# A fused attention and mixture-of-experts layer: other VectorE steps in the routing, places in a group's fourth tile, the fifth group's shared rows in the middle stage, and sums in halves at the end

## What is computed

```python
q = layernorm(x)                                   # eps 1e-5
out = attention(q Wq, ctx Wk, ctx Wv; 16 heads of 64) @ Wo + bo
x = x + (gamma * norm(q + out, eps=1e-3) + beta)
f = layernorm(x)                                   # 4096 tokens
scores = softmax(f @ Wg)                           # 32 experts
weights, indices = top_k(scores, 4)
for e in range(32):                                # at most C = 4 * (4096 * 4) / 32 pairs
    y[tok_e] += silu(f[tok_e] W1[e]) * (f[tok_e] W3[e]) @ W2[e] * w_e    # hidden size 128
z = silu(f Ws1) * (f Ws3) @ Ws2                    # shared, hidden size 256
return x + y + z
```

## Time and profile before

| | before |
|---|---|
| median of 3 runs | 789.82 us (789.68 to 792.14) |
| profiled execution: time, span | 792.1 us, 790.3 us |
| mean TensorE clock granted | 0.981 |
| TensorE matmul, weight load busy | 747.7 us (95%), 596.3 us (75%) |
| VectorE, ScalarE, GpSimd busy | 533.0 us (67%), 465.4 us (59%), 379.6 us (48%) |
| DMA | 164.44 MB, mean 208 GB/s |
| instructions | 18644 |

### The profile page before, as it was taken

One profiled execution on the slowest core, in us unless ns is written; L12 is line 12 of the kernel. 1 busy time (PEld: TensorE's weight loads), 2 busy tenths in 40 slices (PEclk: granted clock), 3 DMA queues, 4 the chain that ended last, 5 costly groups with the idle time before them and its releaser, 6 DMA issues.

```text
span 790.3 us, 18644 instructions
## 1 busy us (share of the span) xinstructions
PE 747.7 (95%) x4222; PEld 596.3 (75%) x4223; DVE 533.0 (67%) x1683; ACT 465.4 (59%) x1820; POOL 379.6 (48%) x352
## 2 busy tenths in 40 slices
PE   6988999999999999999998959999999999999995
PEld 5766777877777877677775648999999999998555
DVE  4854547575959687686977645666666666665588
ACT  2665777777677868566833204666666666666110
POOL 1002242225747574766567663666666665666000
PEclk9998999999999999999999898999999999999999
DMA  9812072325444454489929788777777675664897
GB/s 311 256 41 63 33 223 96 121 94 170 149 150 140 151 179 136 161 261 355 302 95 367 269 312 265 214 218 246 225 235 240 216 245 182 194 189 142 344 409 323
DMA packets 104734, 164.44 MB, mean 208 GB/s; under 512 B 10902, under 2 KB 87780, under 8 KB 103140
## 3 DMA queue, kind: packets, MB, share of 16 engines
q1 hardware_dynamic: 90447, 120.01, 46.2%
q0 software_dynamic: 13824, 41.96, 14.9%
q10 hardware_dynamic: 404, 1.82, 0.7%
HBM read 90.01 MB, written 78.97 MB: 214 GB/s over the span
## 4 chain that ended last, share of the span: by engine, by line
PE 69%; DVE 13%; issue 6%; POOL 5%; ACT 4%; DMA 2%; DVEq 0%; ACTq 0%; SPq 0%; POOLq 0%
PE psum L1750 19%; PE psum L1639 11%; PE psum L1551 11%; PE psum L1757 9%; PE psum L1487 9%; POOL expert_lists L704 4%; PE psum L1671 4%; PE psum L1510 2%; ACT sm L853 2%; PE psum L1597 2%; DVE big L1450 2%; DVE ln1g L1053 1%; PE psum L1525 1%; DMA expert_lists<-rows,slot 1%; PE psum L1686 1%
## 5 line engine op out<-in xcount | busy, mean ns | idle before, releaser
L744 POOL DMA_INDIRECT y_d<-sm,yrow x160 | 155.1, 970 | 105.7 <-DVE yrow L1426 78.2
L1750 PE MATMUL psum<-xbT,w_now 128*128 128x128 f32 x1280 | 171.2, 277 | 0.2
L704 POOL DMA_INDIRECT expert_lists<-rows,slot x128 | 128.7, 1006 | 72.3 <-issue 36.5
L853 ACT ACTIVATE sm<-psum,nmax 128x77 f32<-128x77 f32 x512 | 158.0, 369 | 6.4 <-DVE nmax L1065 6.3
L1750 PEld LDWEIGHTS psum<-xbT,w_now 128*128 128x128 f32 x1280 | 156.8, 193 | 2.7 <-issue 1.8
L722 POOL TENSOR_TENSOR sm<-sm,sinv 128x1232 f32<-128x1232 f32 x32 | 71.9, 2247 | 173.9 <-DVE sinv L1072 173.8
L1639 PE MATMUL psum<-big,pT 128*128 (+1 forms) x640 | 143.6, 379 | 0.0
L1551 PE MATMUL psum<-big,xnT 128*128 (+2 forms) x384 | 140.6, 516 | 0.0
L1639 PEld LDWEIGHTS psum<-big,pT 128*128 128x128 f32 x640 | 119.1, 190 | 15.0
L853 ACT ACTIVATION_READ_ACCUMULATOR sm<-psum,nmax 128x1 f32 x512 | 128.5, 251 | 0.0
L1551 PEld LDWEIGHTS psum<-big,xnT 128*128 128x128 f32 x384 | 71.3, 192 | 57.4 <-issue 51.7
(11 more groups left out here) (191 smaller groups left out, 972.4 us busy)
## 6 DMA issues: line engine op xcount, KB each, us to landing
xblk<-expert_lists SPq DMA_DIRECT2D x160, 160.0 KB, 2.3
y_d<-zero SPq DMA_DIRECT2D x32, 512.0 KB, 3.8
big<-y_d SPq DMA_DIRECT2D x8, 2048.0 KB, 16.1
big<-in_L_ffn_W SPq DMA_DIRECT2D x16, 320.0 KB, 6.7
xin<-in_x SPq DMA_DIRECT2D x36, 128.0 KB, 2.6
xres<-in_x SPq DMA_DIRECT2D x8, 512.0 KB, 5.8
x_d<-x SPq DMA_DIRECT2D x8, 512.0 KB, 3.3
xn2T_d<-xn2T SPq DMA_DIRECT2D x8, 512.0 KB, 2.9
```

Of the source, the lines that this page charges most:

```text
L704: pool.indirect_dma_start(out=lists, out_offset=bass.IndirectOffsetOnAxis(ap=slot[:, ph, tt, k:k + 1], axis=0), in_=rows[:, ph, tt, :], in ...
L744: pool.indirect_dma_start(out=y_d, out_offset=bass.IndirectOffsetOnAxis(ap=yrow[:, q:q + 1], axis=0), in_=eo[:, q, :], in_offset=None).the ...
L853: last = nc.scalar.activation(sm[:, t % 2, h * SK:(h + 1) * SK], head_scores(h, h + 1), ACT.Exp, bias=nmax[:, t % 2, h:h + 1], accum_out=s ...
L1750: last = mm(bank(2 + q % 2)[:, i * P:(i + 1) * P], w_now[:, q % 2, i, k, :], xbT[:, q % 2, k, :], start=k == 0, stop=k == KC - 1)
```

## The change

In the loop: `iota_e`, `topf`, `onehot`, `mask` and the sums of it become bfloat16; the reduce over the four choices becomes two additions of halves (`mask2`, `mask`), and so does the group's sum. The softmax of the router is written straight into the rows' weight columns and is no longer multiplied by the mask. `label_pairs` and `label_rows` become one function: twice the third one-hot plus the second, three times the fourth plus that, plus the pair's number. `place` compares and multiplies in one instruction, and stands behind `invert` in the fourth tile of the group two later (before: in the first tile of the group three later, ahead of that tile's own work). GpSimd issues four of the 16 scatters in that fourth tile, after its additions, and 3, 1, 4 and 4 in the next group's first three tiles.

In the middle stage: the order on VectorE is centring, place, then the first gate; the last group's `label_rows` and `place` stand ahead of the table of blocks. xn2T of the fifth group (MID) is loaded by SP behind its fills, and `s_up(MID, 0)`, `s_down(3)`, `s_up(MID, 1)`, two silus and two gates run there; all engines' blocks wait for these gates. Its `s_down` comes first at the end.

At the end: TensorE adds `base` with one matmul of 512 columns for each half of a group, and for groups 5 and 6 (`BY_PE`) one of the four y rows (`add_rows`). The sums of the first and the last group are made in halves of two tiles, with a load for each half, and a store for each half of the last group. The z banks and the order of gates and sums change.

The core of the diff; left out are buffers that only change their type, the semaphores, waits that follow from the counts, and removed lines that stand in the functions printed above:

```diff
+        BY_PE, IN_HALVES = (MID + 1, MID + 2), (0, NG - 1)
...
@@ -602,6 +617,10 @@
             sp.wait_ge(s["dummy_filled"], 32)
             sp.wait_ge(s["fill_ready"], 1)
             fill_lists(sp, [(0, 8), (8, 16), (16, SP_FILLS)])
+            sp.wait_ge(s["s_psum"], 2 * (MID - 1))
+            sp.wait_ge(s["xn2T_stored"], 16 * (MID + 1))
+            sp.dma_start(xg_end[0], xn2T_d[MID:MID + 1, :, :].rearrange("o p (k n) -> (o p) k n", k=KC)
+                         ).then_inc(ld_xg_first, 16)
             sp.wait_ge(s["tab_ready"], 1)
...
+                y_g = y_d[g * GT * TOPK:(g + 1) * GT * TOPK, :].rearrange("(p t k) d -> p t k d", t=TG, k=TOPK)
+                if g in IN_HALVES:
+                    for half in range(2):
+                        tiles = slice(half * TG // 2, (half + 1) * TG // 2)
+                        sp.dma_start(ysum[:, g % RING, tiles, :, :], y_g[:, tiles, :, :]).then_inc(ld_y_half[half], 16)
+                else:
+                    sp.dma_start(ysum[:, g % RING, :, :, :], y_g).then_inc(ld_y[g % RING], 16)
...
+                if g == NG - 1:
+                    for half in range(2):
+                        tiles = slice(half * TG // 2, (half + 1) * TG // 2)
+                        sp.wait_ge(s["z_added"], 2 * g + half + 1)
+                        sp.dma_start(out_g[:, tiles, :], final[:, g % RING, tiles, :]).then_inc(stored[g % RING], 16)
...
                 jh, ph = ago(j, p, 3)
                 if t == 0 and live(jh, ph):
-                    wait(pool, "rows_ready", (num(jh, ph) + 1) * TG)
-                    wait(pool, "rows_of_y_ready", num(jh, ph) + 1)
-                    wait(pool, "weights_ready", num(jh, ph) + 1)
-                    slots_due(num(jh, ph) + 1)
-                    scatter_rows(jh, ph, 0, 6 if live(j, p) else 1)
+                    scatter_rows(jh, ph, 4, 7 if live(j, p) else 5)
...
                 if t < 3 and live(jh, ph):
-                    scatter_rows(jh, ph, *((6 if live(j, p) else 1, 9), (9, 13), (13, 16))[t])
+                    scatter_rows(jh, ph, *((7 if live(j, p) else 5, 8), (8, 12), (12, 16))[t])
+                j2, p2 = ago(j, p, 2)
+                if t == 3 and live(j2, p2):
+                    wait(pool, "rows_ready", (num(j2, p2) + 1) * TG)
+                    wait(pool, "rows_of_y_ready", num(j2, p2) + 1)
+                    wait(pool, "prob_ready", num(j2, p2) + 1)
+                    slots_due(num(j2, p2) + 1)
+                    scatter_rows(j2, p2, 0, 4)
...
+            shared_silu(MID, 0)
+            shared_silu(MID, 1)

             phase1_over(act)
+            wait(act, "s_gated", 2 * (MID + 1))
...
+                wait(dve, lists_ready[ph], jh * (16 * TG * TOPK))
+                prob = rows[:, ph, :, W_AT:ROW]
...
-                    nc.vector.tensor_reduce(mask[:, :, :], onehot[:, :, :, :].rearrange("p t k e -> p t e k"), AX,
-                                            ALU.add).then_inc(s["mask_ready"], 1)
...
+                    nc.vector.tensor_tensor(mask2[:, :, :, :], onehot[:, :, 0:2, :], onehot[:, :, 2:4, :], ALU.add
+                                            ).then_inc(s["mask2_ready"], 1)
+                    wait(dve, "mask2_ready", g + 1)
+                    wait(dve, "prefix_psum", g)
+                    nc.vector.tensor_tensor(mask[:, :, :], mask2[:, :, 0, :], mask2[:, :, 1, :], ALU.add
+                                            ).then_inc(s["mask_ready"], 1)
+                    wait(dve, "mask_ready", g + 1)
+                    nc.vector.tensor_tensor(gsum2[:, :, :], mask[:, 0:2, :], mask[:, 2:4, :], ALU.add
+                                            ).then_inc(s["gsum2_ready"], 1)
+                    wait(dve, "gsum2_ready", g + 1)
+                    nc.vector.tensor_tensor(gsum[:, :], gsum2[:, 0, :], gsum2[:, 1, :], ALU.add
+                                            ).then_inc(s["gsum_ready"], 1)
+                    wait(dve, "gsum_ready", g + 1)
+                    nc.vector.tensor_tensor(before_sum[:, 1 - ph, :], before_sum[:, ph, :], gsum[:, :], ALU.add
+                                            ).then_inc(s["earlier_ready"], 1)
...
+                    nc.vector.scalar_tensor_tensor(choice2[:, :, :], onehot[:, :, 2, :], 2.0, onehot[:, :, 1, :],
+                                                   ALU.mult, ALU.add).then_inc(s["choice2_ready"], 1)
+                    wait(dve, "choice2_ready", g + 1)
+                    nc.vector.scalar_tensor_tensor(choice[:, :, :], onehot[:, :, 3, :], 3.0, choice2[:, :, :],
+                                                   ALU.mult, ALU.add).then_inc(s["choice_ready"], 1)
+                wait(dve, "choice_ready", g + 1)
...
+                nc.vector.tensor_tensor(rows[:, ph, :, Y_AT:W_AT], choice[:, :, :], over_e(pair[:, :, 0]), ALU.add
+                                        ).then_inc(s["rows_of_y_ready"], 1)
+                wait(dve, "rows_of_y_ready", g + 1)
                 nc.vector.tensor_scalar(pair[:, :, :], pair[:, :, :], float(GT * TOPK), None, ALU.add).then_inc(s["pair_ready"], 1)
...
-                    nc.vector.tensor_reduce(rows[:, ph, :, Y_AT:W_AT],
-                                            pairs_e[:, :, :, :].rearrange("p t k e -> p t e k"), AX, ALU.add
-                                            ).then_inc(s["rows_of_y_ready"], 1)
...
-                nc.vector.tensor_scalar(valid[:, :, :], pos[:, :, :], float(CAP), None, ALU.is_lt
-                                        ).then_inc(s["valid_ready"], 1)
...
+                nc.vector.scalar_tensor_tensor(slot_e[:, :, :], pos[:, :, :], float(CAP), base_e[:, :, :], ALU.is_lt, ALU.mult
+                                               ).then_inc(s["slot_e_ready"], 1)
...

-                if t == 0 and live(*g3):
-                    label_rows(*g3)
-                    place(*g3)
                 if t == 1 and live(*ago(j, p, -1)) and live(j, p):
...
                     third_scale(*g1)
-                if t == 3 and live(*g2):
-                    label_pairs(*g2)
+                if t == 3 and live(*g2) or t == 1 and live(*g2) and not live(j, p):
+                    label_rows(*g2)
...
+                if t == 3 and live(*g2):
+                    place(*g2)
                 if t == 1 and live(*g1):
                     second_norm(*g1)
...

             before_last, last_group = (NG // 2 - 1, 0), (NG // 2 - 1, 1)
-            label_pairs(*before_last)
-            label_rows(*before_last)
             dve.wait_ge(s["pt_psum"], NT * 3)
+            second_center(*last_group)
+            place(*before_last)
             shared_gate(0, 0)
-            place(*before_last)
+            second_scale(*last_group)
             shared_gate(0, 1)
-            second_center(*last_group)
-            second_scale(*last_group)
             residual(*last_group)
...
             mark(*last_group)
-            label_pairs(*last_group)
+            label_rows(*last_group)
+            place(*last_group)

             tab_ops = [0]
...
             tab_op(nc.vector.tensor_scalar(count[:, :], o_ps[:, 0:E], float(CAP), None, ALU.min))
             nc.vector.tensor_tensor(fill_at[:, :], count[:, :], region0[:, :], ALU.add).then_inc(s["fill_ready"], 1)
-            label_rows(*last_group)
-            place(*last_group)
             shared_gate(2, 0)
             shared_gate(2, 1)
...
             nc.vector.tensor_copy(tabp[:, :].bitcast(U8)[:, PACK:PACK + BLOCKS], o_ps[0:3, 0:BLOCKS]
                                   ).then_inc(s["tab_ready"], 1)
+            shared_gate(MID, 0)
             add_shared(3)
+            shared_gate(MID, 1)
...
                 p = g % RING
                 terms = [base[:, g * TG:(g + 1) * TG, :]] if g < MID else []
-                terms += [ysum[:, p, :, k, :] for k in range(TOPK)]
...
+                    nc.vector.tensor_tensor(out_sb[:, tiles, :], term[:, tiles, :], so_far[:, tiles, :], ALU.add
+                                            ).then_inc(s["ysum_step"], 1)
+                    sums_done[0] += 1
...
+            def sum_group(g):
+                if g in IN_HALVES:
                     for half in range(2):
-                        wait(dve, "z_psum", g * 2 + (half + 1))
-                        nc.vector.tensor_tensor(final[:, p, 2 * half:2 * half + 2, :],
-                                                bank(z_bank(g) + half).rearrange("p (t d) -> p t d", t=2),
-                                                so_far[:, 2 * half:2 * half + 2, :], ALU.add).then_inc(s["z_added"], 1)
+                        so_far = sum_rows(g, half, slice(half * TG // 2, (half + 1) * TG // 2))
+                        if g >= MID:
+                            add_z(g, half, so_far)
+                else:
+                    so_far = sum_rows(g, 0, slice(0, TG))
+                    if g >= MID:
+                        add_z(g, 0, so_far)
+                        add_z(g, 1, so_far)
...
-            shared_gate(MID, 0)
```

(34 more changed lines are left out.)

161 lines of the change are left out of this document (85 added, 76 removed).

## The result

The changed kernel takes 801.07 us (median of 4 runs, 798.74 to 802.04), the kernel before beside it 790.64; the ratio is 1.0127, with a 95% interval of 1.0106 to 1.0147. It is slower by 10.4 us, where 3.2 were forecast with a range up to 800. The profiled execution took 802.0, its span is 800.3.

What follows compares the result with a forecast made beforehand. TensorE was taken to bound the kernel (69% of the chain), the change acting at four seams. Loop -2.5, blocks +7.6, end -2.7 make +2.4 on 792.1; with 0.8 less for the loop, 789.8 + 3.2 = 793, range 786 to 800.

Steps and rivals of the forecast that it cites:

- The sign: Whole kernel: slower, by 3.2 us against the median of 789.8; chance of slower 0.53.
- the main mechanism: Middle stage: TensorE waits about 10 us for the xn2T load behind SP's fills, then half clock; blocks +7.6.
- Rival (3): Attention loop: place delays ScalarE's exponentials by more than its 4.16 us of cover; about 801 in all; chance 0.09.
- Loop: Attention loop: shorter TensorE waits for rows, next tile and xn2T, and less half clock: -2.5 us, bounds -6.2 and +3.
- the half-clock stretch: Attention loop: some 3.4 us at half clock behind TensorE's xn2T wait, worth 1.7; a quarter was to go.
- Head of the middle stage: Last group's routing: TensorE waits 1.2 us for the first gate; ScalarE's rows come 0.3 to 0.5 earlier.
- The load: Middle stage: fifth group's xn2T, issued at about 463 behind all 21 SP fills, lands at about 471.
- rival (1): Middle stage: the load does not queue behind the fills, lands at 467; blocks +3.6, total 789; chance 0.17.
- From the landing to the blocks: Middle stage: s_up, s_down, s_up, 2.0 of half clock and 1.8 of silu and gate, from 471 to 485.5.
- The blocks: Expert blocks: start at 485.5, a move of +7.6 after allowing for the 2.0 of half clock they lost before.
- The end: Last stage: halves start earlier and finish sooner, y loads no earlier: -2.7 us, bounds -4.5 and -1.
- Rival (2): Middle stage: load there in time, scatters start the blocks 2.6 earlier at full clock; -9, 781; chance 0.12.

Runs made afterwards that it cites:

- run 9: The changed kernel itself, run again as a control: 802.35 us against 790.55 for the kernel before, ratio 1.0141.
- run 12: Changed kernel with the xn2T load behind the first 8 fills, and the first gates and fills' positions ahead of place: 788.51 us, ratio 0.9974 to the kernel before.
- run 10: Changed kernel with SP's load of the fifth group's xn2T behind the first 8 fills, not all 21: 790.37 us, ratio 1.0004 to the kernel before.
- run 11: Changed kernel with the fifth group's shared part at the end, first gates and fills' positions ahead of place: 787.27 us, ratio 0.9956 to the kernel before.
- run 4: Changed kernel with the first gates ahead of place on VectorE: 890.0 us, ratio 1.0215 to the kernel before.
- run 1: Changed kernel with the fifth group's shared part back at the end: 875.59 us against 873.44 for the kernel before, ratio 1.0029.

## Why the prediction was wrong

The sign and the main mechanism (the load of xn2T behind SP's fills, half clock behind the wait) were as forecast; the size was 3 where 10 was measured. The step that failed first is the time at which that load lands: 5.4 later than forecast. Some 3 to 4 of this were handed on from the head of the middle stage: its wait for the first gate was put at 1.2 and measured 3.29, and in the trace the larger part of that gate's lateness is a hold of VectorE that the prediction looked for at another instruction. The rest is time in the queue. Rival (3) gave 801 and so hits the number, but its mechanism, a longer loop, is not there. Step by step, in the prediction's order, each against the profiled execution:

**Loop**, forecast -2.5: measured -2.8, and -3.0 in run 9. The sum is right by luck, since its misses cancel: of TensorE's waits the one for rows is 2.4 (1.0 of 2.5 was to go), the one for the next tile 1.1 (0.9 of 1.5 was to go) and the one for xn2T 0.4, while the half-clock stretch of 1.7 went whole and not by a quarter (the clock is 1.00 from 310 to 400). The listing by line (shortest, median and longest in ns, first and last start in us) of place's step with two SBUF inputs and of the small norm step of the earlier trace rows:

```profile
L1296 DVE SCALAR_TENSOR_TENSOR slot_e<-pos,base_e x8: 293/2295/2303, 175.5 to 441.1; 128x128 f32<-128x128 f32 x8
...
L1091 DVE TENSOR_SCALAR ln1g<-ln x9: 154/171/1699, 24.4 to 365.2; 128x8 f32<-128x8 f32 x5, 128x8 f32 x4
```

place's step takes 2.30 beside GpSimd's scaling and 0.29 in the middle stage: held for 2.0, as the rule of the Trainium skill that the prediction cited says (SBUF — State Buffer, "Who interferes with whom"). No wait of TensorE came of it: ScalarE's 4.16 us of waiting for TensorE are still there (at 277.10), and the loop is shorter, so rival (3) falls. The norm's step shrank from 3.9 at the most to 1.70, the 2 us forecast; but it has a single input by its line, so the rule in the form that the prediction gave does not explain it.

**Head of the middle stage**, forecast a wait of 1.2 for the first gate: measured 3.29, with 8 matmuls at half clock behind it, 1.7 more (5.31 against 3.60). The trace names the load of xn2T as releaser, but this is a later event of a semaphore that was long up; VectorE's gate ended at 415.24, s_up(1,0) began at 415.39:

```profile
410.75 1.66 DVE L1168 SCALAR_TENSOR_TENSOR scaled<-res,mv,gamma_b 128x256 f32<-128x256 f32 x4
412.32 0.28 DVE L1292 TENSOR_TENSOR base_e<-pos,region 128x128 f32<-128x128 f32 x1
...
414.56 0.68 DVE L1375 TENSOR_TENSOR sm<-sm,psum 128x512 f32<-128x512 f32 x1
```

VectorE had kept step with TensorE up to here: TensorE's first s_up and VectorE's router maxima both stand 5.8 earlier than before (2.8 by the loop, 3.0 by the execution). Then one of VectorE's steps with two SBUF inputs came to lie beside GpSimd's addition of beta:

```profile
400.97 2.93 DVE L1219 TENSOR_TENSOR lexp<-logits,lmax 128x128 f32<-128x128 f32 x1
```

```profile
401.38 2.36 POOL L756 TENSOR_TENSOR xres<-xres,beta_b 128x1024 f32<-128x1024 f32 x1
```

It ended at 403.90, 0.16 behind that addition, and took 0.29 in the kernel before, where the addition was over at 405.64 and this step began at 406.77. Runs 9 to 12 have it at 2.91 to 3.02, beside the same addition. The prediction looked for this hold at place alone and expected of beta's addition only that it would be over sooner; counted from the first router matmul it starts 1.1 later here. Against the first s_up the gate ends 3.7 later than before (10.8 and 7.0): 2.6 by this hold, the other 1.1 by the new order on VectorE. No run takes the hold alone away. ScalarE's rows began at 428.43, right behind silu(1,1), and the norm they need was there at 424.5. So rows came 25.2 and not 21.5 after the first s_up. This is the first failed term: 3.7 us. With the first gates and the fills' positions moved ahead of place, and the hold still there, run 12 against run 10 gave back 3.5 of it in rows and 2.9 in the start.

**The load**, forecast to land 322.3 after the first router matmul (471 less the loop's 2.5): measured 327.6 and 327.8, in run 9. Of these 5.4, 3 to 4 are the fills' later start (SP 301.3 and 300.3 after that matmul, forecast 297.4), which is the head's term handed on, and 1.4 to 2.5 the queue (26.3 and 27.5 from the first fill to the landing, forecast 25.0). It landed 9.2 and 10.1 after its issue and not 3.8, the median of the earlier trace rows: rival (1) falls, and run 10 shows that the load's place behind the fills is the cause. This agrees with what the Trainium skill says of rings in DMA: Bandwidth & Descriptors, "Queues, rings and completion order", but no run here shows the order of one ring by itself.

**From the landing to the blocks**, forecast 14.5: measured 16.0 and 14.5. **The blocks**, which the sum made 2.0 shorter because the half clock would lie ahead of them: 253.5 and 252.1 against 253.3. The changed profile shows the half clock a second time (0.66 in its first 5 us), behind the last 2.24 of waiting for the gate; run 9 has full clock there and 1.2 of the 2.0.

**The end**, forecast -2.7: measured -1.2 and -1.5. The loads took the same 47.7 from the first issue to the last landing as before (745.2 to 792.9; 734.0 to 781.6), as forecast. Behind the landing 7.4 are left of 8.7, where about 6 (8.7 less 2.7) were forecast: VectorE's second half stands behind the first, which waits 1.65 for group 3's store, queued behind group 7's loads. The fifth group's earlier shared part is worth nothing there: run 11 without it and run 10 with it both have 59.7. TensorE's waits of 4.1 and 1.3 for gates, queued on VectorE behind sum_group(0), took its place. The forecast of 784.85 for the last addition is also 0.4 more than its own terms give (781.6 + 3 x 0.72 + 0.69 = 784.45).

The terms that failed, from the profiled forecast of 794.5: +5.4 for the load, +1.5 for landing to blocks, +2.2 for the blocks, +1.5 for the end, -0.3 for the loop, -3.0 for the part ahead of it give 801.8, and 802.0 was measured. In run 9 the same terms are +5.5, 0, +0.8, +1.2, -0.5 and +0.4, which gives 801.9, and 802.35 was measured: the load's term is the one that stays, the terms of the clock and of the stretch ahead change with the execution. Rival (2) fell for the reason given, but was an edit of one line away: in run 10 the load is there in time, and the total is the kernel before's.

## What to carry to other kernels

A load that is moved to an earlier stage must be placed in the queue's order as well as in the engine's: ask what its queue still has to issue ahead of it, and put it in as soon as its buffer is free, between the bulk transfers. When an edit shifts VectorE's and GpSimd's work against each other, look at every VectorE step with two SBUF inputs that comes to lie beside a long GpSimd addition, and not only at the step that was moved: place was held for 2.0 us under cover, and a step that nobody had touched was held for 2.6 where a gate, the rows, the fills and the load stood behind it. Work that leaves a stage bound by DMA may give nothing there (the end took 59.7 with the fifth group's part and without it), so price the move by the stage that it enters.

## What was not expected of the hardware

The same kernel takes 790 us on some chips and 871 to 879 on four others. Single instructions are as long on both (VectorE's small steps 0.16, ScalarE's silu 0.60, TensorE's 8 matmuls of s_up 3.60); what grows is the time between them, 0.04 to between 0.5 and 1.2 in VectorE's chain above, and the block stage goes from 253 to between 307 and 323. TensorE is busy for 86.7 of 87 us from 143 to 230 on both kinds, and for 79.9 and 79.4 of 80 from 230 to 310. Why was not found. It is not a matter of loops against written-out code: all of ScalarE's attention groups and VectorE's first four are written out and run alike on both kinds, while the blocks are a loop and are slower. Nor is it the chip alone, since run 4 has the chain at 0.2 on the chip where run 1 has it at 0.7 to 1.4. It turned orders round: with place in the fourth tile the loop was 6.6 to 9.7 us longer on these chips than with place in the first, all of it behind 310 us.

TensorE's clock was no function of the gap's length alone. Behind 12.0 us it was 0.50, behind 3.63 (run 11) 0.50, behind 3.29 0.66 in the window. Behind the 1.81 ahead of the rows the prediction expected full clock: the router's 16 matmuls took 2.56, between the 1.97 of the loop and the 3.46 of before, and s_down behind them 6.53, the 6.44 of before. In run 9, behind the same 1.81, the router took 1.99 and s_down 4.08, with 1.00 granted. Behind 2.24 ahead of the first block it was 0.66 in the first five us of the changed kernel's profile, and 1.00 in run 9's, which has the same gap.
